# Attention lead of a fused kernel: bias of the values on GpSimd, values projected between score tiles, heads normed in other steps

## What is computed

```python
x1 = _ln(x) * (scale1 + 1.0) + shift1
qkv_bias = jnp.concatenate([q_bias, jnp.zeros_like(q_bias), v_bias])
qkv = (x1 @ mat_qkv_w.T + qkv_bias).reshape(B, L, 3, H, hd)
q, k, v = [jnp.transpose(qkv[:, :, i], (0, 2, 1, 3)) for i in range(3)]
sm = jnp.exp(jnp.minimum(scale_mul, MAX_SCALE_MUL))
q = _l2norm(q) * sm          # x / max(|x|, 1e-12) for each head
k = _l2norm(k)
scores = jnp.einsum('bhqd,bhkd->bhqk', q, k)
probs = jax.nn.softmax(scores, axis=-1)
o = jnp.einsum('bhqk,bhkd->bhqd', probs, v)
```

## Time and profile before

| | |
|---|---|
| median of 3 runs | 3171.84 us (3170.88 to 3175.58) |
| profiled execution | 3174.25 us, its span 3172.5 us |
| TensorE busy | 3097.2 us (98%) |
| VectorE busy | 2759.5 us (87%) |
| ScalarE busy | 2703.8 us (85%) |
| GpSimd busy | 2484.2 us (78%) |
| mean granted clock of TensorE | 0.992 |

### The profile page before, as it was taken

How to read it: one execution, slowest core, us unless ns; L and a number is a source line. 1 busy time by engine, 2 the same in 40 slices (tenths; PEclk the granted TensorE clock), 3 DMA queues, 4 the chain that set the end, 5 groups by cost and what they waited for, 6 DMA issues and landing times.

```text
span 3172.5 us, 59515 instructions
## 1 busy us (share of the span) xinstructions
PE 3097.2 (98%) x23304; PEld 2631.1 (83%) x23304; DVE 2759.5 (87%) x3049; ACT 2703.8 (85%) x4496; POOL 2484.2 (78%) x638
## 2 busy tenths in 40 slices
PE   8999999999999999999999999999999999999999
PEld 6998899884699889988479988998848998888965
DVE  3999999977499999997659999999666999999963
ACT  3999999974699999995579999999558999999845
POOL 2999999971199999996139999999415999999910
PEclk9999999999999999999999999999999999999999
DMA  5222222210222232221022232223102223222100
GB/s 185 80 84 67 85 73 84 74 56 29 74 69 82 74 92 68 82 85 65 1 84 67 82 87 79 74 82 89 46 14 80 81 76 89 69 74 82 57 14 8
DMA packets 195240, 225.69 MB, mean 71 GB/s; under 512 B 77449, under 2 KB 149641, under 8 KB 193681
## 3 DMA queue, kind: packets, MB, share of 16 engines
q1 hardware_dynamic: 194960, 221.89, 22.8%
HBM read 217.37 MB, written 4.48 MB: 70 GB/s over the span
## 4 chain that ended last, share of the span: by engine, by line
PE 82%; POOL 8%; issue 4%; DVE 3%; ACT 1%; DMA 0%; SPq 0%; DVEq 0%; ACTq 0%; POOLq 0%
PE bank L1129 23%; PE bank L1109 17%; PE bank L1009 11%; PE bank L1110 10%; POOL states L674 5%; PE bank L1105 4%; PE bank L1353 4%; POOL y_gated L674 3%; PE bank L1390 2%; PE bank L1493 2%; PE bank L1378 2%; DVE states L1640 2%; PE bank L1184 1%; PE bank L1136 1%; PE bank L1281 1%
## 5 line engine op out<-in xcount | busy, mean ns | idle before, releaser
L674 POOL TENSOR_TENSOR states<-states,c_rows 128x2048 f32<-128x2048 f32 x336 | 1531.6, 4574 | 132.4 <-DVE states L1640 129.9
L1640 DVE TENSOR_TENSOR_SCAN states<-decay,bank 128x512 f32<-128x512 f32 x1376 | 1577.4, 1201 | 16.5 <-ACT decay L854 1.2
L854 ACT ACTIVATE decay<-dt,a_log 128x512 f32<-128x512 f32 x2048 | 1305.5, 710 | 0.0
L845 ACT ACTIVATE inflow_tok<-dtx_tok,b_tok 128x512 f32<-128x512 f32 x1536 | 995.7, 713 | 85.7 <-PE bank L1110 74.6
L1109 PE MATMUL bank<-ident,inflow_tok 128*128 128x128 f32 x5280 | 904.7, 280 | 35.8 <-DVE states L1640 18.7
L1129 PE MATMUL bank<-ident,states 128*128 128x128 f32 x5504 | 826.0, 273 | 6.1 <-DVE y_gated L1646 3.0
L1640 DVE TENSOR_TENSOR_SCAN y_gated<-decay,bank 128x512 f32<-128x512 f32 x672 | 777.1, 1202 | 14.0 <-ACT decay L854 5.0
L674 POOL TENSOR_TENSOR y_gated<-y_gated,c_rows 128x2048 f32<-128x2048 f32 x168 | 768.4, 4574 | 19.8 <-DVE y_gated L1640 18.1
L1109 PEld LDWEIGHTS bank<-ident,inflow_tok 128*128 128x128 f32 x5280 | 598.9, 141 | 205.7 <-issue 87.6
L1110 PE MATMUL bank<-b_diag,dtx_tok 128*128 128x128 f32 x3520 | 681.3, 275 | 0.0
L1129 PEld LDWEIGHTS bank<-ident,states 128*128 128x128 f32 x5504 | 645.0, 141 | 14.3 <-POOL states L674 7.8
(11 more groups left out here) (174 smaller groups left out, 2592.3 us busy)
## 6 DMA issues: line engine op xcount, KB each, us to landing
c_rows<-c_spill SPq DMA_DIRECT2D x256, 512.0 KB, 3.7
b_diag<-diag_ring SPq DMA_DIRECT2D x256, 128.0 KB, 2.3
xproj_w<-in_xproj_w SPq DMA_DIRECT2D x32, 320.0 KB, 3.8
in_w<-in_in_w SPq DMA_DIRECT2D x16, 512.0 KB, 4.5
out_w<-in_out_w SPq DMA_DIRECT2D x4, 1024.0 KB, 8.2
in_w<-in_fc_w SPq DMA_DIRECT2D x8, 512.0 KB, 4.3
xproj_w<-in_w SPq DMA_DIRECT2D x8, 512.0 KB, 4.7
xproj_w<-in_fc_w SPq DMA_DIRECT2D x4, 1024.0 KB, 4.7
```

Source lines behind the costliest of these rows:

```text
L674: pool.tensor_tensor(state_row, state_row, c_row.to_broadcast([P, KI, L]), ALU.mult).then_inc(weighed, PAIRS)
L845: last_tok = act.activation(inflow_tok[:, r % SLOTS, t, :], dtx_tok[:, d, t, :], ACT.Copy, scale=b_tok[:, d, t, s:s + 1])
L854: act.activation(decay[:, r % SLOTS * KI + k, :], dt[:, d, k, :], ACT.Exp, scale=a_neg[:, d, k, s:s + 1]).then_inc(decay_ready, 1)
L1640: dve.tensor_tensor_scan(state_slots[r % STATES][:, k, time], decay[:, slot, time], banks[k % INFLOW_BANKS][:, time], 0.0, ALU.mult, ALU.a ...
```

## The change

On TensorE the four products that bring the values' bias go away. The values' tiles leave their place behind the queries and keys and stand after score tiles 9, 11, 13 and 15, in banks 6 and 7, once all heads are turned and copied out. Queries and keys get a bank for each tile (4, 5, 0, 1), and a tile's projection follows right behind its turned rows. ScalarE squares before it copies the keys, and squares tile 0 before it shifts tile 3. Guard and scale become one instruction ahead of the inversion (the scale's inverse is prepared once). The heads of tiles 0 to 2 are multiplied by GpSimd, those of tile 3 by VectorE. GpSimd adds the bias to the copied values. The diff, cut to its core:

```diff
+V_AT = (9, 11, 13, 15)
-QK_BANK = 4
+QK_BANKS = (4, 5, 0, 1)
...
+                for t in range(TT - 1):
+                    pool.wait_ge(k_ready, b * TT + t + 1)
+                    pool.wait_ge(norm_inv_ready, b * TT + t + 1)
+                    pool.tensor_tensor(heads(qk_pad[:, t, :, :].rearrange("p g c -> p (g c)"), LANE)[:, :, 0:HD],
+                                       heads(qk[:, t, :], HD), norm_inv[:, t, :].unsqueeze(2).to_broadcast([P, 2 * H, HD]),
+                                       ALU.mult).then_inc(qk_unit, 1)
+                for i in range(2):
+                    values = v_ones[:, 2 * i:2 * i + 2, :, 0:HD]
+                    pool.wait_ge(v_ready, b * 2 + i + 1)
+                    pool.tensor_tensor(values, values, heads(row_b[:, V_BIAS, :], HD).unsqueeze(1).to_broadcast([P, 2, H, HD]),
+                                       ALU.add).then_inc(v_biased, 1)
+
                 pool.wait_ge(res_ready, (b * 2 + 1) * TT)
-                pool.wait_ge(qk_unit, (b + 1) * TT)
...
+            def square(b, t):
+
+                bank = banks[QK_BANKS[t]]
+                act.wait_ge(q_ready, b * TT + t + 1)
+                act.activation(qk_sq[:, t, D:2 * D], bank[:, D:2 * D], ACT.Square)
+                act.activation(qk_sq[:, t, 0:D], qk[:, t, 0:D], ACT.Square).then_inc(sq_ready, 1)
+                act.activation(qk[:, t, D:2 * D], bank[:, D:2 * D], ACT.Copy).then_inc(k_ready, 1)
...
+                square(b, 1)
+                head_root(0)
+                square(b, 2)
+                head_root(1)
+                square(b, 3)
+                head_root(2)
+                head_root(3)
...
+                def heads_tile(t):
+
                     ln_wait(b, 2, t)
-                    pe.wait_ge(res_ready, (b * 2 + 1) * TT + t + 1)
                     if t > 1:
-                        pe.wait_ge(k_ready, b * TT + t - 1)
+                        pe.wait_ge(res_ready, (b * 2 + 1) * TT + t - 1)
...
+                ln_turn(b, 2, 1)
+                heads_tile(0)
+                ln_turn(b, 2, 2)
+                heads_tile(1)
+                ln_turn(b, 2, 3)
+                heads_tile(2)
+                heads_tile(3)
 
                 def value_tile(t):
 
-                    to = banks[V_BANK + t // 2][:, t % 2 * D:(t % 2 + 1) * D]
-                    pe.matmul(to, ident[0:1, 0:1].to_broadcast([1, P]), row_b[0:1, V_BIAS, :], start=True, stop=False,
-                              skip_group_check=True)
+                    to = banks[TURN_BANK + t // 2][:, t % 2 * D:(t % 2 + 1) * D]
+                    pe.wait_ge(qk_t_ready, (b + 1) * (2 * NG - 1))
...
-                for t in range(TT):
-                    value_tile(t)
...
+                    if j == 0:
+                        pe.wait_ge(v_biased, (b + 1) * 2)
...
+                    if u in V_AT:
+                        value_tile(V_AT.index(u))
                     if u == STEPS + LEAD_BANKS - 1:
                         pe.wait_ge(qk_t_ready, (b + 1) * (2 * NG - 1))
+                        pe.wait_ge(v_ready, (b + 1) * 2)
                         turn_q_max(0, banks[7])
...
+                def invert(t):
                     dve.wait_ge(norm_ready, b * TT + t + 1)
...
+                    dve.scalar_tensor_tensor(norm_over[:, t, :], norm[:, t, :], EPS_NORM, inv_scale[:], ALU.max,
+                                             ALU.mult).then_inc(norm_over_ready, 1)
+                    dve.wait_ge(norm_over_ready, b * TT + t + 1)
+                    dve.reciprocal(norm_inv[:, t, :], norm_over[:, t, :]).then_inc(norm_inv_ready, 1)
...
+                dve.wait_ge(k_ready, (b + 1) * TT)
+                dve.wait_ge(norm_inv_ready, (b + 1) * TT)
+                dve.tensor_tensor(heads(qk_pad[:, TT - 1, :, :].rearrange("p g c -> p (g c)"), LANE)[:, :, 0:HD],
+                                  heads(qk[:, TT - 1, :], HD), norm_inv[:, TT - 1, :].unsqueeze(2).to_broadcast([P, 2 * H, HD]),
+                                  ALU.mult).then_inc(qk_unit_last, 1)
```

More of the change, by code:

```diff
@@ L377, in build @@
         k_ready = sem("k_ready")
+        v_biased = sem("v_biased")
         v_ready = sem("v_ready")
@@ L424, in build, with heads @@
         out_rows = out.rearrange("b (t p) d -> b p t d", p=P)
+        def heads(row, e):
+            return row.rearrange("p (h e) -> p h e", e=e)
         def lead_last(bank):
@@ L784, in ln @@
                 shift(0)
+                if i == 2:
+                    root(2)
+                    shift(1)
+                    root(3)
+                    shift(2)
+                    square(b, 0)
+                    shift(3)
+                    return
                 shift(1)
@@ L864, in _ @@
                     act.wait_ge(sign_ready, 1)
-                    act.activation(qk_scale[:, 0:H], scale_cap[:], ACT.Exp).then_inc(q_scale_ready, 1)
+                    act.activation(inv_scale[:, 0:H], scale_cap[:], ACT.Exp, scale=-1.0).then_inc(inv_scale_ready, 1)
                 prepare(0, 0, s)
@@ L895, in batch, with head_root @@
                 ln(b, 2)
-                def root(t):
+                def head_root(t):
                     act.wait_ge(norm_sq_ready, b * TT + t + 1)
                     act.activation(norm[:, t, :], norm_sq[:, t, :], ACT.Sqrt).then_inc(norm_ready, 1)
[L901 to L913, removed]
+                square(b, 1)
[5 more added lines that the diff above has]
+                head_root(3)
                 for i in range(1, 2 * NG):
@@ L918, in batch @@
                     act.activation(to, banks[TURN_BANK + i % 2], ACT.Copy).then_inc(qk_t_ready, 1)
+                act.wait_ge(ones_ready, b + 1)
+                for i in range(2):
+                    act.wait_ge(v_mm, b * TT + 2 * i + 2)
+                    act.activation(v_ones[:, 2 * i:2 * i + 2, :, 0:HD],
+                                   banks[TURN_BANK + i].rearrange("p (t h e) -> p t h e", t=2, e=HD), ACT.Copy).then_inc(v_ready, 1)
                 def lanes(g):
@@ L1723, in batch @@
                     dve.wait_ge(sign_ready, 1)
-                for t in range(TT):
-                    dve.wait_ge(qk_mm, b * TT + t + 1)
-                    dve.tensor_tensor(qk[:, t, 0:D], banks[QK_BANK + t % 2][:, 0:D], row_b[:, Q_BIAS, :],
-                                      ALU.add).then_inc(q_ready, 1)
-                    if t:
-                        sum_squares(t - 1)
-                    if t > 1:
-                        unit(t - 2)
-                sum_squares(TT - 1)
-                unit(TT - 2)
@@ L1734, in batch @@
-                unit(TT - 1)
+                query(0)
+                query(1)
+                sum_squares(0)
+                query(2)
+                sum_squares(1)
+                invert(0)
+                query(3)
+                sum_squares(2)
+                invert(1)
+                sum_squares(3)
+                invert(2)
+                invert(3)
+                dve.wait_ge(k_ready, (b + 1) * TT)
[3 more added lines that the diff above has]
+                                  ALU.mult).then_inc(qk_unit_last, 1)
```

54 lines of the change are left out of this document (18 added, 36 removed).

## The result

The changed kernel takes 3194.5 us (median of 6 runs, 3184.3 to 3210.6) against 3173.7 us (6 runs, 3170.9 to 3178.1): ratio 1.0067, interval 1.0039 to 1.0096. It is slower, inside the range given (3164 to 3204), 14.5 us above the forecast of 3180. Its runs differ by 0.8%, those of before by 0.2%. The profiled execution took 3199.15 us, its span 3197.1 us, the mean granted clock 0.986 (0.992 before).

The account below looks back on a forecast made before the run. TensorE bounds the lead up to the first score tile, then VectorE's reductions. Per batch -3.45 + 3.6 - 1.3 = -1.15, plus 3.0 and 0.3 for the clock, gives +2.15, +8.6 in four: 3180 us, range 3164 to 3204.

Parts of the forecast that it names:

- TensorE's value work hides the norm's chain: In each batch's lead, TensorE's value work covers the norm of the heads almost exactly; removing it leaves that chain bare.
- First score tile 3.45 us earlier: In batch 0's lead, the first score tile starts at 739.9 instead of 743.36, a gain of 3.45 us a batch.
- nearest row: The one profile row at hand for a GpSimd product of this size, 1.27 us, taken for its products of the heads.
- rival 3: GpSimd is slower on strided heads, 1.7 us a product, +1.1 us in each of four batches: 3184 us; chance 0.08.
- Four waits of 0.9 us beside the values: VectorE waits 0.9 us before each of tiles 10, 12, 14 and 16: 3.6 us lost a batch.
- The rival in which values fit beside the reductions: The values cost nothing beside VectorE's reductions: 3166 us with the clock's fall, 3153 without; chance 0.10.
- The wait after tile 21 goes: TensorE's work is ready before VectorE needs tile 22, so the wait there goes: 1.3 us gained a batch.
- The clock falls in each batch, 3.0 us lost in a spell of 6.8: After TensorE's empty stretch of 4.2 us before the turns, its clock falls to 0.50 for 6.8 us: 3.0 us lost.
- rival 1: The clock holds, or falls without harm: -1.15 us a batch, -4.6 in all, 3167 us; chance 0.20.
- rival 2: Half clock lasts through the values: 8 us a batch on the forecast, 3212 us in all batches, 3196 in two; chance 0.17.
- 0.3 of the sum: Estimate for a second clock fall in the thin stretch behind tile 16: 0.3 us lost a batch, bounds 0 and 1.6.
- the forecast's own range: 3173 to 3188 us around the forecast of 3180, from the bounds of the half-clock spell; chance 0.45.

Follow-up runs that it names:

- Experiment 5: The kernel before with only the four bias products of the values left out: 3191.45 us, ratio 1.0056.
- experiment 1: The changed kernel with ten filling products on TensorE between the last projection and the turn of the heads: 3173.85 us, ratio 0.9999 against the kernel before.
- experiment 3: The changed kernel with all four products of the heads on VectorE, none on GpSimd: 3204.7 us, ratio 1.0096 against the kernel before.
- experiment 10: The changed kernel, values back before the turn, GpSimd multiplying only tiles 0 and 1, its bias additions held until VectorE's last product: 3170.9 us.
- experiment 11: The kernel before with one filling product behind each of score tiles 10, 13, 16 and 19: 3168.1 us, ratio 0.9984.
- experiment 7: The changed kernel with values back before the turn of the heads and GpSimd multiplying only tiles 0 and 1: 3191.2 us, ratio 1.0060 against the kernel before.

## Why the prediction was right, and where its sizes were off

- **TensorE's value work hides the norm's chain, and the chain will lie bare.** Right. Experiment 5 takes 2.5 us of TensorE's work away, and VectorE's last product ends 14.96 us behind the first projection with and without it.
- **First score tile 3.45 us earlier.** Off: 1.9 to 2.5, and 2.8 with the clock held (experiment 1: 16.8 to 14.0). The projections came as worked out (3.45 for the last two). GpSimd was faster than its nearest row (1.06 us instead of 1.27), but the sum lacked a term: VectorE's guard took 0.79 us instead of 0.18 and its product 1.50 or 1.21 instead of 0.69 while GpSimd ran, so that VectorE's product, and not GpSimd's third, ended last. Experiments 3 and 10 show the cause from two sides: without GpSimd beside them the same instructions take 0.18 and 0.69. A GpSimd that is slower itself (rival 3) was the wrong worry.
- **Four waits of 0.9 us beside the values.** Right: 0.83 each. B at full clock is 24.95 us against 21.3 (experiments 1 and 11), 3.6 us. The rival in which values fit beside the reductions did not come; it comes at three tiles apart, where 0.24 is left.
- **The wait after tile 21 goes.** Right: it went in batches 0, 2 and 3, and 1.08 us was left in batch 1, where the clock was low. That it had been the clock's is shown by experiment 11.
- **The clock falls in each batch, 3.0 us lost in a spell of 6.8.** The mechanism was right in all four batches; its size was too small. The spells took 10.2, 37.5, 6.8 and 10.2 us. By the table less the clean 14.0 + 24.95, they cost 3.6, 15.7, 2.8 and 4.4 us, and 1.1 more in batch 3, where a second spell reached the periods: 6.9 us a batch where 3.3 were put. The failed estimate is the one for the mean spell: it took the likeliest for all four, and left the spell that lasts through the values as a rival at 0.17, for all batches or two. It came in one of four, with some 12 us, and that one batch is most of the distance in the profiled execution, from 3182.9 to 3199.15. The runs from 3184 to 3211 fit none, one or two of such batches in an execution; that each run is so made up is argued, not shown.
- **With the clock held the sum is -1.15 us a batch (rival 1).** Measured by experiment 1, batch 2: 42.1 us against 42.6 for the mean of before, -0.5, the collision's 0.7 in it.
- **The price of the long spell (rival 2).** Too low. It put 8 us a batch on the forecast, with the thin score tiles less than doubled by half clock. In batch 1 they nearly doubled as well: two score tiles take 2.08 us where at full clock they take 1.13, and a pair with values 4.02 instead of 2.12. With the turns (two waits of 2.03 instead of 0.2) that batch cost some 12.7 more than the forecast's 3.0.

Together the four batches of the profiled execution come to -0.5 and 6.9, +6.4 us a batch, against the -1.15, 3.0 and 0.3 of the sum. Direction and mechanism were right. The median of 3194.5 lies above the forecast's own range (3173 to 3188); it is inside the whole range because that range made room for rival 2.

The page TensorE: Matmul & The Clock Gate of the Trainium skill (Why this matters for your kernels) warned of idle gaps between bursts of matmuls; experiments 1 and 5 agree with it in direction, from both sides, 20 and 18 us. They differ in size: in experiment 5 single waits of 1.52 and 1.11 us with transposes between them were enough, shorter than the gaps of which the page warns, as was the wait of 1.86 us in the earlier trace rows, and the measurement decides.

The page SBUF — State Buffer of the Trainium skill (Who interferes with whom) says that a VectorE instruction with two inputs in SBUF and a GpSimd instruction that reads SBUF take turns at a shared port, whole instruction by whole instruction. The prediction had not drawn on it, and with it the missing term was there to be found. Experiments 7 and 10 agree: 1.26 us against 0.18 for such an instruction, while sums and inversions with one input kept 0.63 to 0.68 and 0.35 us beside the same GpSimd instructions.

What stays open: why the clock came back after 7 us in one batch and after 37 in another, with the same order of work. The batches differ in where the spell began within it; what decides it was not tried by itself.

## What to carry to other kernels

Work of an engine that looks free to remove or move may be what hides another engine's chain, and on TensorE it also holds the clock: before taking it out, look at what is left in that stretch, and price the stretch behind it at half clock. If a hole stays, a few products into a free bank are worth more than they cost (here 0.65% in front of the turns of the changed kernel, experiment 1, and 0.16% in the score tiles of the kernel before, experiment 11). Before giving an idle GpSimd work beside VectorE's critical chain, look for instructions of VectorE with two inputs in SBUF next to it; order the rest of GpSimd's work behind that chain.

## What the runs showed of the hardware

- A VectorE instruction with two SBUF inputs that meets one of GpSimd's seems to stand until that one is over: 0.18 became 0.79 and 1.26 us, 0.69 became 1.21 to 1.50. The guard ends 0.05 us and the product some 0.55 us behind the end of GpSimd's instruction (changed kernel, batches 0 and 1). Inversions and sums beside the same GpSimd instructions kept their times.
- The clock stayed at 0.50 for 37.5 us in one go, through turns, score tiles and value products, with TensorE busy for 36.3 of the window's 37.4 us.
- GpSimd's product in which each factor serves 16 neighbouring elements took 1.06 us for 128x512; its bias addition and its gate product of the same size, with one operand repeated in blocks of 256, took 1.27.
